# A graph network's kernel: the counting row of its selectors moved from SBUF to PSUM

## The reference

```
ew = edge_attr @ edge_w + edge_b
inv_cnt[i] = 1 / max(segment_sum(type == i, dst), 1)
for l in range(3):
    msg = relu(x[src] * ew)
    out = x @ roots[l] + biases[l]
    for i in range(3):
        h = segment_sum(msg * (type == i), dst) * inv_cnt[i]
        out = out + h @ weights[l, i]
    x = x + relu(out)
return layernorm(x_first + x)
```

## Time and profile before

| | |
|---|---|
| median of 3 runs | 3102.99 us (3097.03 to 3103.08) |
| profiled execution, its span | 3632.0 us |
| its mean granted TensorE clock | 0.895 |
| PE busy | 2818.6 us, 78% |
| DVE busy | 2148.2 us, 59% |
| POOL busy | 2256.5 us, 62% |
| ACT busy | 1285.0 us, 35% |
| DMA engines, mean rate | 124 GB/s |

### The profile page before, as it was taken

One profiled execution on the slowest core, in us unless ns is written; L12 is line 12 of the kernel. 1 busy time (PEld: TensorE's weight loads), 2 busy tenths in 40 slices (PEclk: granted clock), 3 DMA queues, 4 the chain that ended last, 5 costly groups with the idle time before them and its releaser, 6 DMA issues.

```text
span 3632.0 us, 59677 instructions
## 1 busy us (share of the span) xinstructions
PE 2818.6 (78%) x18430; PEld 2609.9 (72%) x18430; DVE 2148.2 (59%) x5997; ACT 1285.0 (35%) x2700; POOL 2256.5 (62%) x2368
## 2 busy tenths in 40 slices
PE   6777778888888777778777877777777777787777
PEld 5777777777777677777777777767666777777776
DVE  6666666666666555555555555545555665556566
ACT  6555555555555322222222222222222222222222
POOL 6666666666666466666666666646666666666664
PEclk9999999999999878888898888887888888888888
DMA  4444444444444344444444444434444444444443
GB/s 126 128 129 128 127 132 127 131 127 131 130 128 130 114 125 118 122 119 121 122 124 118 124 122 119 122 106 127 125 126 121 130 123 127 129 124 130 125 128 100
DMA packets 318631, 450.88 MB, mean 124 GB/s; under 512 B 155996, under 2 KB 205802, under 8 KB 318314
## 3 DMA queue, kind: packets, MB, share of 16 engines
q0 software_dynamic: 112608, 307.65, 29.8%
q1 hardware_dynamic: 205706, 139.36, 13.7%
HBM read 401.96 MB, written 44.82 MB: 123 GB/s over the span
## 4 chain that ended last, share of the span: by engine, by line
PE 61%; issue 16%; another core or an unknown queue 9%; DVE 8%; ACT 3%; DVEq 2%; POOL 1%; DMA 0%; POOLq 0%; SPq 0%
PE bank L800 31%; PE bank L781 14%; PE bank L849 13%; DVE acc L971 4%; PE bank L754 2%; DVE t L988 1%; DVE xg L1088 1%; ACT at L656 1%; PE bank L824 1%; ACT oh_a L702 1%; PE bank L795 1%; DVEq L1078 1%; DVEq L971 1%; DVE S L952 0%
## 5 line engine op out<-in xcount | busy, mean ns | idle before, releaser
L608 POOL DMA_INDIRECT xg<-x,idx x1564 | 1490.9, 953 | 897.3 <-issue 361.5
L800 PE MATMUL bank<-S,xg 128*128 128x96 f32 x9384 | 1459.0, 305 | 400.7 <-issue 197.4
L800 PEld LDWEIGHTS bank<-S,xg 128*128 128x128 f32 x9384 | 1324.2, 217 | 461.2 <-issue 441.2
L685 ACT ACTIVATE xg<-xg 128x512 f32<-128x512 f32 x1173 | 739.1, 630 | 2064.0 <-DVE xg L1088 1270.0
L971 DVE TENSOR_TENSOR acc<-acc,bank 128x192 f32 x2346 | 817.1, 348 | 767.0 <-PE bank L800 490.6
L1088 DVE TENSOR_TENSOR xg<-xg,bank 128x512 f32<-128x512 f32 x1173 | 802.0, 684 | 600.2 <-remote 273.5
L781 PE MATMUL bank<-wsb,at 128*128 128x256 f32 x4692 | 990.4, 338 | 213.8 <-issue 128.8
L608 POOL DMA_INDIRECT xg<-in_x_dram,idx x782 | 750.5, 960 | 451.0 <-PE bank L800 212.2
L781 PEld LDWEIGHTS bank<-wsb,at 128*128 128x128 f32 x4692 | 753.8, 214 | 286.7 <-issue 183.5
L849 PE MATMUL bank<-W,acc 128*128 128x256 f32 x1764 | 506.5, 411 | 2.2 <-issue 2.0
L849 PEld LDWEIGHTS bank<-W,acc 128*128 128x128 f32 x1764 | 385.5, 257 | 5.6 <-issue 2.0
(11 more groups left out here) (87 smaller groups left out, 728.2 us busy)
## 6 DMA issues: line engine op xcount, KB each, us to landing
at<-attr_t SPq DMA_DIRECT2D x390, 128.0 KB
xg<-x,idx POOLq DMA_INDIRECT x1564
attr_t<-at SPq DMA_DIRECT2D x195, 128.0 KB
xg<-in_x_dram,idx POOLq DMA_INDIRECT x782
hs<-in_edge_attr_dram SPq DMA_DIRECT2D x195, 64.0 KB
x<-t SPq DMA_DIRECT2D x96, 128.0 KB
xblk<-x SPq DMA_DIRECT2D x96, 128.0 KB
xblk<-in_x_dram SPq DMA_DIRECT2D x48, 128.0 KB
```

Source lines behind the costliest of these rows:

```text
L608: eng.indirect_dma_start(out=xg[:, n % XR, :], out_offset=None, in_=xs[l], in_offset=bass.IndirectOffsetOnAxis(ap=idx[:, tile(j):tile(j) + ...
L685: eng.activation(v, v, ACT.Relu).then_inc(s_r, 1)
L800: last = eng.matmul(pA[V % 2][:, 192 * i + 96 * h:192 * i + 96 * h + 96], xg[:, n % XR, 128 * h:128 * h + 128], S[:, slot(l, 2 * q + i), : ...
```

## The change

The counting row, columns 0 to 147 of `iota`, is copied once into bank 5 of PSUM (as float32) by DVE before the loops, and both comparisons read it from there. The second operand, `kr` or `hb`, and the outputs stay in SBUF. The count products, which had bank 5, go to columns 400 to 402 of the collecting bank of their step, which L795 and L800 leave free, and `count` gets a wait on the sums that were last read from that bank.

```diff
+        steps_of = bank[5][:, 0:148]
...
             def count(k):
-
+                V = starts[k]
+                eng.wait_ge(s_acc, min(NT, 2 * (V - 1)))
                 if k == 0:
                     eng.wait_ge(s_df, 4)
                 else:
                     eng.wait_ge(s_inv, 2 * k - 1)
                 eng.wait_ge(s_cn, min(NP, starts[k] - 1))
-                eng.matmul(pH[:, 4 * (k % 2):4 * (k % 2) + 3], diff[:, :], cnt[:, 3 * blocks[k]:3 * blocks[k] + 3],
+                eng.matmul(pA[V % 2][:, 400:403], diff[:, :], cnt[:, 3 * blocks[k]:3 * blocks[k] + 3],
                            start=True, stop=True).then_inc(s_cm, 1)
...
+            link(eng.tensor_copy(steps_of, iota[:, :]))
...
-                eng.tensor_tensor(S[:, at4:at4 + w, :], iota[:, 1:WK + 1].unsqueeze(1).to_broadcast([128, w, WK]),
+                eng.tensor_tensor(S[:, at4:at4 + w, :], steps_of[:, 1:WK + 1].unsqueeze(1).to_broadcast([128, w, WK]),
                                   kr[:, c:c + w].unsqueeze(2).to_broadcast([128, w, WK]),
                                   ALU.is_equal).then_inc(s_S, 1)
...
-                                      iota[:, 1 + f:1 + f + HW].unsqueeze(1).to_broadcast([128, w, HW]),
+                                      steps_of[:, 1 + f:1 + f + HW].unsqueeze(1).to_broadcast([128, w, HW]),
...
-                    eng.tensor_scalar(v, pH[:, 4 * (k % 2):4 * (k % 2) + 3], 1.0, None, ALU.max).then_inc(s_inv, 1)
+                    eng.tensor_scalar(v, pA[starts[k] % 2][:, 400:403], 1.0, None, ALU.max).then_inc(s_inv, 1)
```

## The result

The kernel after takes 3022.24 us (3021.01 to 3023.61) against 3102.41 us: a ratio of 0.9751, 95% interval 0.9734 to 0.9768, 80 us faster. The forecast was 3077 us in a range from 3035 to 3107. The sign and the mechanism held, the size did not.

The account below looks back on a forecast made before the run. The prediction took POOL's gathers as the nearest limit of the unprofiled run, PE behind. Stretch -26, copy +0.3, comparison duration 0 and count wait 0 took 3102.99 us to 3077 us, range 3035 to 3107.

Parts of the forecast that it names:

- POOL as the nearest limit of an unprofiled run, with a floor of 3014.8 us: 2346 gathers 1.25 us apart plus start, end and layer pauses: 3014.8 us, 88.2 us below the median; PE behind.
- L952 with two SBUF inputs stretches a gather, and a PSUM source does not: Gathers starting during L952 take 1.27 us instead of 0.95; reading its row from PSUM would remove that.
- Duration of the comparisons: 0: L952 and L957 reading the row from PSUM: no change in their own duration, bounds -3 to +45 us.
- Rival D: PSUM reads slow L952 and L957 by up to 45 us, 3148 us if all on the path; chance 0.05.
- The size of the stretch, 26 us: Gathers' time beyond 946 ns each: 22.1 us in the trace, scaled by 1/0.854 to 26 us saved.
- the far end: Upper bound on the stretch saved: all 588 L952 cost 0.32 us each, 188 us, limited to 88.2 us.
- the ceiling of 88.2 us: Median 3102.99 us less POOL's floor of 3014.8 us: the most that removing the gathers' stretch could return.
- case A: POOL is on the unprofiled run's path and the stretches come back: 3077 us, range 3015 to 3096; chance 0.50.
- The copy, 0.3 us: Copying the counting row into bank 5 once before layer 0: 0.3 us, bounds 0.2 and 0.5.
- The count's wait costs nothing: L812's new wait on L971's sums, 49 times: 0 us, at most 13.7 us if PE always arrived early.
- Rival C: PE reaches the count before the later L971 ends: +13.7 us, 3117 us, POOL's gain hidden; chance 0.07.
- Rival B: Stretches are real but hidden by the 12-tile ring, a steady PE step setting the time: 3103 us; chance 0.38.

Follow-up runs that it names:

- extra_two_sbuf: Kernel after plus a second, overwritten comparison ahead of each one writing S, its counting row read from SBUF; 3085.60 us, ratio 0.9961.
- extra_one_sbuf: Kernel after plus a second, overwritten comparison ahead of each one writing S, its counting row read from PSUM; 3021.01 us, ratio 0.9756.
- row_f32_sbuf: Kernel before with the counting row as float32, still in SBUF, counts left in bank 5; 3097.29 us, ratio 0.9992.
- counts_only: Kernel after without the copy: counts moved with their new wait, both comparisons reading the SBUF row; 3097.53 us, ratio 0.9995 to the kernel before.
- before_again: Kernel before, unchanged, run for a profile as long as its timed runs; 3099.45 us, ratio 1.0008.

## Why the prediction was right in kind and short in size

- *POOL as the nearest limit of an unprofiled run, with a floor of 3014.8 us.* Right that POOL is the limit. The kernel after takes 3022.24 us, 7.4 us above that floor, and 6.0 us of these are the stretch that is left (2225.3 - 2219.3). That the floor fits this well is luck in part. It leaves out 7.6 us in which POOL fills other tiles before the 13th gather, at 36.9 us. Against that, the pauses between layers (22.2 and 18.15 us) are 4.6 us shorter than the ones it took from the longer execution, and the time from the last gather's start to the end (23.4 us, from 2998.4 to 3021.8) is 3.4 us shorter.
- *L952 with two SBUF inputs stretches a gather, and a PSUM source does not.* Right, shown both ways by extra_two_sbuf and extra_one_sbuf, and by place against type in row_f32_sbuf. Only the wording "waits until L952 has ended" is too simple: held gathers end 0.82 us after that end, where a whole gather would take 0.946 us. The Trainium skill ("SBUF — State Buffer", who interferes with whom) infers that a tensor_tensor leaves descriptor generation alone; the runs do not agree, since the gather, whose work on POOL is to issue an indirect DMA, takes 1.30 us against 0.95. Its rule on two SBUF inputs, in the same section, agrees with them.
- *Duration of the comparisons: 0.* Right: 550 against 553 ns and 197 against 201. Rival D, slower through the PSUM read, is out.
- *The size of the stretch, 26 us: the step that failed.* The prediction said "I take the average that the trace shows, 26 us, over it", having worked out 22.1 us from a trace 529 us longer than the median and scaled it by the density of starts alone, a factor of 1/0.854 = 1.17. Measured in an execution of normal length it is 78.9 us, of which 72.9 us went. Both things that the scaling held fixed had changed: the comparison held 231 gathers instead of 110, and each for 0.31 instead of 0.18 us. The prediction had argued itself that in a POOL-bound run L952 follows the landing at a fixed distance, so that the hit repeats, and it used that only for the far end. The new trace shows it: nearly the same offset, 0.07 and 0.08 us, at 1393.92 and 1399.28, and 147 gathers at 0.05 to 0.15 us after a comparison where the longer execution had 17. A third term would have been at hand: the two L952 in the earlier trace rows cost 0.09 and 0.32 us, 0.205 us in the mean; times 588 that is 121 us, which the ceiling of 88.2 us cuts off. The measured mean is 72.9 / 588 = 0.12 us. The measured time lies inside the span that the prediction gave to its own case A (3015 to 3096 us), but it had called the part below 3035 us less likely than one in ten and left it out.
- *The copy, 0.3 us.* Right, 0.32 us once:

```profile
26.01 0.32 DVE L946 CAST bank<-iota 128x148 f32<-128x148 bf16 x1 [1.03 <-ACT hb L644]
```

- *The count's wait costs nothing.* Right, by counts_only and by the row that answers to the earlier trace rows:

```profile
493.46 0.35 DVE L974 TENSOR_TENSOR acc<-acc,bank 128x192 f32 x1
...
494.39 0.28 PE L814 MATMUL bank<-cnt,diff 128*128 128x3 f32 x2
...
494.53 0.19 PE L796 MATMUL bank<-oh_b,oh_a 128*128 128x12 bf16 x2
```

  The sum L974 ends at 493.81, the count starts 0.58 us later and L796 directly after it. That lead is half of the 1.16 us of the earlier trace rows, and it suffices; the shortest of the 49 in this trace is 0.46 us. Rival C, slower through the new wait, is out.
- *Rival B, hidden by the ring.* Out for the timed runs. It fits the trace that was at hand, whose POOL waited 762 us; in the executions of normal length POOL starts each gather 0.30 us after the end of the one before, and the two pauses between layers are its only long waits.

What made the first profiled execution 529 us longer is open; no run here repeated it. Its granted TensorE clock was 0.895, against 0.951 in before_again, and PE was busy for 163.9 us more (2818.6 against 2654.7); that is less than a third of the 529 us.

## What to carry to other kernels

Before a profile is used for sums, compare its span with the timed runs: this one, 17% longer, had another bound, and its means of waits and stretches were those of the other bound. Work out the floor of each engine from its closest spacing (here 2345 x 1.25 us and the pauses) and ask what lengthens exactly that spacing. The gap to the floor is a bound on the prize and not the prize itself; in this one case, with the floor within 3% of the median, the gap of 88.2 us was nearer to the 80 us gained than the 26 us from the odd trace. Where one event can fall into step with another, as the comparison did with the gathers, a mean over another execution says little: ask what it costs when it hits every time. A VectorE instruction that is cheap, and hidden in the idle time of its own engine, can still cost the kernel time if both its input tensors lie in SBUF while GpSimd issues gathers and GpSimd sets the time. In this kernel two remedies worked: one input moved to PSUM (3022.24 us), or the instruction moved to a time between two starts (3048.02 us).

## What was not expected of the hardware

The hold goes both ways by a few hundredths of a microsecond: a gather that starts 0.07 us after the comparison is held (1.30 us instead of 0.95), one that starts 0.03 us after it is not, and the comparison takes 0.62 instead of 0.55 us. The two losses are unlike: the gather loses up to 0.4 us and ends 0.82 us after the comparison, while the comparison loses at most 0.08 us. And the account is nearly exact: in nine profiles the span less the gathers' busy time lies between 793.2 and 796.5 us.
